# Layer 0 distances: the square root on VectorE by two Heron steps instead of GpSimd's pow, ScalarE's second squares ahead of an eviction

## What is computed

```
q_dst = Q[dst] + rel_q[type];  k_src = K[src] + rel_k[type] + (edge_attr_32 @ Wt + bt)
euclid = sum(q_dst * k_src, per head) / sqrt(16) * decay
man_dist = norm(m[src] - m[dst])          # m: nodes in the hyperbolic ball, one number per edge
hyp = -hyp_beta * man_dist * decay
logits = alpha * euclid + (1 - alpha) * hyp
attn = softmax of logits over the edges of one destination
agg = segment_sum(v_src * attn);  then out projection, layer norm, FFN, layer norm
```

## Time and profile before

| | |
|---|---|
| median of 3 runs | 4499.23 us |
| the runs | 4487.35, 4502.24, 4499.23 us |
| profiled execution: span from first to last instruction | 4484.2 us |
| profiled execution: its own time | not given apart; the lowest run is 3.2 us above the span |
| busy in the span: PE, DVE, ACT, POOL | 76%, 74%, 47%, 42% |
| mean granted TensorE clock | 0.876 |
| layer 0's gathers | 808, first start 164.5 us, last 1604.4 us |
| GpSimd's pow (line 1229) | 101, each 1636 to 1792 ns |

### The profile page before, as it was taken

The page is one execution under the profiler, slowest core; times in us unless marked ns, Lnnn a source line. Parts: engine busy times, 40 slices in busy tenths (PEclk is TensorE's granted clock), DMA queues, the critical chain, the costliest instruction groups (busy, mean ns, idle before and its releaser), DMA issues.

```text
span 4484.2 us, 86419 instructions
## 1 busy us (share of the span) xinstructions
PE 3388.1 (76%) x31445; PEld 2760.2 (62%) x31445; DVE 3298.9 (74%) x6627; ACT 2085.6 (47%) x6042; POOL 1894.4 (42%) x2179
## 2 busy tenths in 40 slices
PE   1388888778989863266663778868699999869996
PEld 1155555545555542166663678855599999859995
DVE  5477776657777754599995887776766666779997
ACT  2355555545666532288883557660222222234443
POOL 0366677757777751000000210000255555548884
PEclk6688898889999976677876889989899999989998
DMA  4666676667777740100001220114244443223332
GB/s 96 210 189 182 189 201 188 188 165 203 223 210 215 211 119 14 39 9 12 12 10 32 90 68 38 46 46 158 82 126 126 125 127 125 88 68 128 129 128 67
DMA packets 382872, 524.57 MB, mean 117 GB/s; under 512 B 78756, under 2 KB 309862, under 8 KB 382304
## 3 DMA queue, kind: packets, MB, share of 16 engines
q1 hardware_dynamic: 328287, 354.60, 26.1%
q0 software_dynamic: 54144, 164.25, 12.9%
HBM read 407.61 MB, written 111.07 MB: 116 GB/s over the span
## 4 chain that ended last, share of the span: by engine, by line
PE 35%; DVE 28%; POOL 14%; issue 9%; ACT 7%; DMA 3%; another core or an unknown queue 2%; SPq 2%; DVEq 0%; POOLq 0%; ACTq 0%
POOL arena_a L1191 11%; PE psum L3700 5%; PE psum L3716 4%; PE psum L3651 4%; PE psum L3649 4%; PE psum L3003 3%; POOL arena_c L1229 2%; ACT arena_c L2966 2%; PE psum L3616 2%; PE psum L3675 2%; PE psum L3288 2%; PE psum L3698 2%; DVE arena_a L3196 2%; PE psum L3647 2%
## 5 line engine op out<-in xcount | busy, mean ns | idle before, releaser
L1191 POOL DMA_INDIRECT arena_a<-src_table,src_tix x808 | 820.4, 1015 | 459.8 <-issue 380.6
L3420 POOL TENSOR_SCALAR node_hot<-arena_c 128x128 fp32r<-128x128 f32 x575 | 369.4, 653 | 900.7 <-DVE arena_c L3308 568.0
L3438 DVE SCALAR_TENSOR_TENSOR msg_parts<-psum,msg_parts 128x512 fp32r<-128x512 f32 (+2 forms) x644 | 425.2, 660 | 260.5 <-ACT msg_parts L3587 228.3
L3138 POOL TENSOR_SCALAR node_hot_dst<-arena_c 128x128 fp32r<-128x128 f32 x587 | 383.9, 671 | 122.1 <-DVE arena_c L3542 67.6
L3587 ACT ACTIVATE msg_parts<-psum 128x512 fp32r<-128x512 f32 (+2 forms) x325 | 186.4, 574 | 520.6 <-PE psum L3651 520.6
L3003 PE MATMUL psum<-arena_a,arena_c 128*128 128x150 f32 x1800 | 288.7, 330 | 173.7 <-ACT arena_c L2969 173.7
L3649 PE MATMUL psum<-arena_c,arena_a 128*128 128x128 bf16 x3675 | 406.4, 220 | 0.0
L3651 PE MATMUL psum<-arena_c,arena_a 128*128 128x128 bf16 x3675 | 406.4, 220 | 0.0
L3003 PEld LDWEIGHTS psum<-arena_a,arena_c 128*128 128x128 f32 x1800 | 283.1, 224 | 176.8 <-ACT arena_c L2969 176.8
L3128 POOL TENSOR_SCALAR arena_a<-arena_a,arena_c 128x2500 bf16<-128x2500 bf16 x8 | 60.0, 7500 | 709.0 <-DMA arena_a<-bucket_lists 709.0
L1371 ACT ACTIVATE arena_c<-psum 128x272 f32<-128x272 f32 x404 | 151.4, 393 | 432.2 <-remote 233.8
(11 more groups left out here) (594 smaller groups left out, 10190.3 us busy)
## 6 DMA issues: line engine op xcount, KB each, us to landing
y_rows<-arena_c SPq DMA_DIRECT2D x101, 576.0 KB
arena_a<-bucket_rows SPq DMA_DIRECT2D x150, 384.0 KB
arena_b<-near_keys SPq DMA_DIRECT2D x101, 252.0 KB
arena_a<-bucket_rows SPq DMA_DIRECT2D x50, 448.0 KB
arena_a<-bucket_lists SPq DMA_DIRECT2D x25, 896.0 KB
pair_counts<-arena_c SPq DMA_DIRECT2D x25, 800.0 KB
arena_a<-bucket_lists SPq DMA_DIRECT2D x25, 704.0 KB
arena_a<-src_table,src_tix POOLq DMA_INDIRECT x808
```

The source lines that it names most:

```text
L1191: e.indirect_dma_start(out_, None, table, bass.IndirectOffsetOnAxis(ap=idx, axis=0)).then_inc(sem, 16)
L3138: return e.tensor_scalar(node_hot3[at % RING_H][:, i, :], iota_row, dst_lo[:, b, t:t + 1], None, ALU.is_equal)
L3420: return e.tensor_scalar(node_hot[at % RING_M][:, i, :], iota_row, src_lo[:, b, 2 * k + j:2 * k + j + 1], None, ALU.is_equal)
L3438: e.scalar_tensor_tensor(out=to[:, 1, 0:nt, :], in0=bank[at % 4][:, 0:nt * P].rearrange("p (t f) -> p t f", f=P), scalar=0.0, in1=to[:, 0, ...
```

## The change

It has four parts. The root of d2 is taken by DVE: a first guess from the bits of the number (half of them plus a constant), then twice Heron's step, guess + d2/guess, with the division as reciprocal and multiply; the factors of one half are gathered in constants. GpSimd takes no root. Its wait for the buffer of d2 is now for the squares. On ScalarE the second group of squares of i1 stands ahead of the second eviction of i3. The guess and the first reciprocal stand ahead of line 1881, the rest behind it.

```diff
 # pool_l0_windows
                     if n >= RING:
                         e.wait_ge(g.gs_used, n - RING + 1)
-                        e.wait_ge(g.dist_ready, n - RING + 1)
+                        e.wait_ge(g.squares, 2 * (n - RING + 1))
                     for t in range(TPB):
-                        if t == 3 * TPB // 4 and n >= 2:
-                            pool_w_distances(e, n - 2)
                         pool_gather(e, GS[n % RING][:, t, :], ...)
-                elif n - 2 < NBLK:
-                    pool_w_distances(e, n - 2)
-        def pool_w_distances(e, k):
-            d2 = small[k % 2][:, 1, 0:TPB]
-            if k == 0:
-                e.wait_ge(g.l0_prep, 2)
-            e.wait_ge(g.squares, 2 * k + 2)
-            e.tensor_tensor(d2, d2, half_row, ALU.pow).then_inc(g.dist_ready, 1)
 # act_l0_windows
+                if b1:
+                    act_w_squares(e, i1, 1)
                 if b3:
                     act_sums(e, i3, D + H, 1, 0, y_stored(i3, 0), SUM_BANKS_W)
-                if b1:
-                    act_w_squares(e, i1, 1)
 # dve_l0_windows (the memset of half_row goes too)
+        ROOT_BITS, ROOT_TRIM = 532380000.0, 1.0 - 3.0691295e-4
                     own.mark(e.tensor_reduce(v3(eu), GS[i1 % RING][:, :, 0:D]..., AX, ALU.add))
+                    guess, other = small[s1][:, 1, TPB:2 * TPB], small[s1][:, 1, 2 * TPB:3 * TPB]
+                    e.wait_ge(g.squares, 2 * i1 + 2)
+                    own.step(e.tensor_scalar(guess.bitcast(I32), d2.bitcast(I32), 0.5, ROOT_BITS, ALU.mult, ALU.add))
+                    own.mark(e.reciprocal(other, guess))
                 if b0:
                     dve_w_low(e, i0)
                 if b1:
-                    e.wait_ge(g.dist_ready, i1 + 1)
+                    own.settle()
+                    own.mark(e.tensor_tensor(other, other, d2, ALU.mult))
+                    own.mark(e.tensor_tensor(v3(eu), v3(eu), bc(hrow[:, 1, :], 1, TPB), ALU.mult))
+                    own.settle()
+                    own.step(e.tensor_tensor(guess, guess, other, ALU.add))
+                    own.step(e.reciprocal(other, guess))
+                    own.step(e.tensor_tensor(other, other, d2, ALU.mult))
+                    own.step(e.scalar_tensor_tensor(out=guess, in0=guess, scalar=0.25 * ROOT_TRIM ** 2, in1=other, op0=ALU.mult, op1=ALU.add))
                     if i1 >= 2:
                         e.wait_ge(g.rows_pe, i1 - 1)
-                    own.step(e.tensor_tensor(v3(t1), bc(d2, 2, H), bc(hrow[:, 2, :], 1, TPB), ALU.mult))
-                    own.step(e.tensor_tensor(v3(eu), v3(eu), bc(hrow[:, 1, :], 1, TPB), ALU.mult))
+                    own.step(e.scalar_tensor_tensor(out=v3(t1), in0=bc(guess, 2, H), scalar=1.0 / ROOT_TRIM, in1=bc(hrow[:, 2, :], 1, TPB), op0=ALU.mult, op1=ALU.mult))
                     e.tensor_tensor(lg, eu, t1, ALU.subtract).then_inc(g.logits_ready, 1)
```

More of the change, by code:

```diff
@@ L557, in program @@
         minus_place = weights0[:, 8 * D:8 * D + 1]
-        half_row = weights0[:, 8 * D + NBLK:8 * D + NBLK + TPB]
         keys_i = arena_a[:, 0:5 * TC * P].bitcast(I32).rearrange("p (k c f) -> p k c f", k=5, c=TC)
@@ L1886, in dve_l0_windows @@
             e.tensor_tensor(minus_place, minus_place, iota_col, ALU.subtract)
-            e.memset(half_row, 0.5)
             e.memset(wd2_wide, 0.0)
```

## The result

The change made the kernel slower: 4782.4 us (median of four, 4759.89 to 4795.88) against 4500.73 for the kernel before on the same chip, ratio 1.063 [1.059, 1.067]. I had forecast 4602 us. The profiled execution, the longest of the four, took 4795.88 us with a span of 4794.1. Layer 0 holds nearly the whole difference: from the start of its last messages to the end the profiles show 2857.7 us, and 2855.2 before.

The account below looks back on a forecast made before the run. The prediction took a ring in layer 0 as the bound: DVE's messages release TensorE, whose keys release DVE's tail. Stretch terms summed to +103 us on the median 4499.23, giving 4602 us; 8-in-10 range 4475 to 4640.

Parts of the forecast that it names:

- DVE's tail longer by 1.25 us per block: Seven small DVE instructions between key comparison and next messages lengthen each block by 1.25 us, at shortest 0.9, at most 1.45.
- No wait for the squares: DVE's wait for ScalarE's squares, ahead of the guess, is covered by L1922 (1.2 us) and costs nothing.
- The moved eviction costs 0: ScalarE's eviction, about 1 us later, hides behind TensorE's filler multiplies: 0, bounds -0.1 and +0.3 us per iteration.
- GpSimd is behind DVE's messages in the first and third stretch, so it only becomes idler: In two of layer 0's three stretches GpSimd waits for DVE, so removing its 1.67 us pow per block only adds idle time.
- the sum: Layer 0's added time: third stretch +52 us, first +21, second +21, the 11 other iterations +9, together +103 us.
- The key wait is bound to the messages, 3.06 us: DVE's waits for TensorE's keys and the pow, together 3.06 us per third-stretch iteration, follow the messages and absorb no added work.
- TensorE answers early: Rival, 16%: once GpSimd no longer sets the pace, keys come without wait and TensorE's length rules: -90 us, 4410 us.
- The lower clock, at most 13 us: TensorE's granted clock, falling in the third stretch, may add 0.3 us to each of 42 iterations, +13 us.
- The shared lock, 4577: Rival, 4%: the pow locks DVE out of the shared SBUF port; its removal gives back up to 25 us, 4577 us.

Follow-up runs that it names:

- run 3: The kernel before, pow and waits kept, with DVE's seven small instructions added on a constant row: 4586.56 us, ratio 1.019.
- run 14: The kernel before with only ScalarE's new order, the second group of squares ahead of the second eviction: 4487.67 us, ratio 0.999.
- run 4: The kernel after the change with ScalarE's old order, the second group of squares behind the second eviction: 4739.01 us, ratio 1.053.
- run 2: The kernel before with GpSimd's pow left out and nothing in its place, logits made from squared distances: 4644.65 us, ratio 1.033.
- runs 5 and 6: Idle pow on GpSimd after each block's third gather: in the changed kernel, 4478.2 us; in the kernel before, beside its own pow, 4527.09 us.

## Why the prediction was wrong

- *DVE's tail longer by 1.25 us per block:* right. 1.18 in the iteration above; run 3 alone gives 87 us, with the pow kept.
- *No wait for the squares:* right. L1914 never waited.
- *The moved eviction costs 0:* right in the kernel before (run 14), 46 us in the changed one (run 4 against the change, 0.0103 of 4500), or 0.46 us per iteration where my bound was 0.3; the two ratios' intervals leave some 20 to 70 us.
- *"GpSimd is behind DVE's messages in the first and third stretch, so it only becomes idler":* this is the step that failed. It was true of GpSimd's own time and blind to what its stream does to others. Taking the pow away cost 147 us by itself (run 2), where I had counted a gain. With a break of the same length put back the sum held nearly: 14.2 us per iteration in the third stretch, as forecast, 16.0 in the first for 15.9, 14.9 in the second for 14.7, and a ratio of 1.017 where 4602 stands for 1.023.
- *The key wait is bound to the messages, 3.06 us:* I had taken it for TensorE's length. Its record ended 4.4 us before the keys came in the earlier trace rows, 7.4 in the iteration after (4.0 and 4.9 on average). The row "<-remote" in the earlier trace rows named no engine for 99.7 of 110.2 us, and I didn't ask why.
- *The early keys of the earlier trace rows, which I put down to a saturated GpSimd (rival "TensorE answers early", 4410):* wrong in its condition. A GpSimd with more idle time made them later. Early keys do come where a break falls right (runs 5 and 6), and then another wait takes much of the gain.
- *The lower clock, at most 13 us:* it fell further, to 0.85. The late keys don't hang on it, since they come at the same place at 1.00 and at 0.50; what it costs elsewhere isn't separated.
- *The shared lock, 4577:* the rule would have given time back when the pow went; run 2 lost 147 us, though it can't separate the two. The trace of before can: L1881 started inside a pow 49 times, and took 0.41 or 0.42 us each time. The same page of the Trainium skill (SBUF — State Buffer, section "SBUF: two separate sides") says that TensorE's and ScalarE's accesses never wait for anyone. No run here contradicts it for the memory's ports; but completions of TensorE did wait while GpSimd issued gathers, so the rule can't be read as "TensorE is undisturbed by GpSimd".

## What to carry to other kernels

Before an operation is taken off an engine that also issues gathers, ask what passes while it runs: its break in the stream may be what lets another engine's results through. Compare the end of the producer's record with the start of the consumer; several us between them with the releaser "remote" may not be the producer's work. And test the removal alone, leaving the result out: that one run (2) would have given the sign and more than half of the size.

## What was not expected of the hardware

- With gathers of 128 rows issued every 1.25 us, the second keys came 4.9 us on average and up to 7.6 us after the end of TensorE's record. ScalarE's and DVE's completions were prompt: TensorE started 0.14 us after ScalarE's eviction ended and 0.06 us after DVE's messages did. A third of the bytes per gather changed little.
- Most often the keys came 1.7 to 2.2 us after the last gather's issue had ended, at either clock of TensorE.
- Behind the third gather, 0.19 us more between two gathers didn't help the time, 0.95 us more mostly, 1.58 us more took the key wait to 0.25 us. What the signals wait for isn't shown.
- A pow on GpSimd took 1.67 us for 128x8 and 1.05 us for 128x4; seven memsets of 128x8, 0.12 us each, 0.33 us together.
